# A fused recommendation tower: early casts and a cast-free start of unit 1, moved marks, and 34 idle turns on TensorE before the first lookup

## The reference

```python
e = stack([tbl_f[ids[:, f]] for f in range(26)], axis=1)        # 2048 x 26 x 128
combined = concatenate([dense[:, None, :], e], axis=1)          # 27 vectors of 128
inter = einsum('bfd,bgd->bfg', combined, combined)              # all dot products
z = concatenate([dense, inter[:, iu0, iu1]], axis=1)            # 351 pairs, i < j
h = concatenate([z, dense], axis=1)                             # 128 + 351 + 128 = 607
h = relu(h @ W_top1 + b_top1)                                   # 512
h = relu(h @ W_top2 + b_top2)                                   # 256
y = h @ W_top3                                                  # 1
```

## Time and profile before

| what | value |
|---|---|
| median of 3 runs | 389.83 us (389.62 to 391.64) |
| the profiled execution: time, span | 391.7 us, 390.0 us |
| TensorE busy | 367.0 us, 94% of the span |
| VectorE, ScalarE, GpSimd busy | 268.3, 190.6, 267.1 us |
| mean granted TensorE clock | 0.994 |
| indirect gathers | 278, 953 ns each on GpSimd, median 2.6 us from issue to landing |
| moved | 35.51 MB, mean 91 GB/s |

### The profile page before, as it was taken

The page is one execution under the profiler, slowest core; times in us unless marked ns, Lnnn a source line. Parts: engine busy times, 40 slices in busy tenths (PEclk is TensorE's granted clock), DMA queues, the critical chain, the costliest instruction groups (busy, mean ns, idle before and its releaser), DMA issues.

```text
span 390.0 us, 7774 instructions
## 1 busy us (share of the span) xinstructions
PE 367.0 (94%) x3094; PEld 360.2 (92%) x3094; DVE 268.3 (69%) x275; ACT 190.6 (49%) x424; POOL 267.1 (68%) x287
## 2 busy tenths in 40 slices
PE   1997998799999999999999999999999999999996
PEld 1786987799999999999999999999999999999996
DVE  5698866979686677819686676828687676832451
ACT  1479346356533565346623455436633465426643
POOL 7777767777777777777677777777677777775000
PEclk9999999999999999999999999999999999999999
DMA  6974821444334332433324342343334342321000
GB/s 229 328 213 93 251 84 51 93 90 82 74 82 96 74 95 56 95 81 77 76 76 102 68 103 56 91 87 76 76 70 104 70 96 62 82 56 42 2 2 1
DMA packets 23004, 35.51 MB, mean 91 GB/s; under 512 B 6252, under 2 KB 16748, under 8 KB 22968
## 3 DMA queue, kind: packets, MB, share of 16 engines
q0 software_dynamic: 8896, 18.24, 19.9%
q1 hardware_dynamic: 13976, 16.77, 16.1%
q10 hardware_dynamic: 96, 0.00, 0.0%
HBM read 34.98 MB, written 0.01 MB: 90 GB/s over the span
## 4 chain that ended last, share of the span: by engine, by line
PE 89%; ACT 4%; DVE 4%; issue 2%; DMA 1%; SPq 0%; DVEq 0%
PE l_ps L387 31%; PE g_ps L417 28%; PE t_ps L396 7%; PE h_ps L429 6%; PE h_ps L431 5%; PE h_ps L430 5%; PE l_ps L379 2%; DVE onehot L604 2%; PE h_ps L476 2%; PE t_ps L425 1%; ACT hot_high L731 1%; DMA hot_idx<-in_hot_ids 1%; DVE zf L634 1%; ACT g_ps L738 1%; ACT xT L752 1%
## 5 line engine op out<-in xcount | busy, mean ns | idle before, releaser
L352 POOL DMA_INDIRECT emb<-in_tbl,idx x278 | 264.9, 953 | 89.7 <-issue 74.1
L604 DVE TENSOR_TENSOR onehot<-hot_idx,rows_ps 128x2048 fp32r<-128x2048 int32 x69 | 155.8, 2283 | 7.5 <-PE l_ps L379 3.2
L417 PE MATMUL g_ps<-xT 128*123 128x108 f32 x1024 | 116.6, 271 | 1.6 <-issue 0.8
L417 PEld LDWEIGHTS g_ps<-xT 128*123 128x123 f32 x1024 | 113.7, 188 | 2.0 <-issue 2.0
L387 PE MATMUL l_ps<-onehot,hot_low 128*128 128x256 f32 x528 | 77.7, 290 | 3.6 <-DVE onehot L604 1.7
L387 PE MATMUL l_ps<-onehot,hot_high 128*128 128x256 f32 x528 | 74.8, 285 | 0.0
L772 ACT COPY zg<-g_ps 27x216 f32<-27x216 f32 x160 | 52.6, 329 | 44.9 <-PE g_ps L417 43.8
L387 PEld LDWEIGHTS l_ps<-onehot,hot_low 128*128 128x128 f32 x528 | 68.3, 193 | 5.0 <-ACT xT L752 2.4
L387 PEld LDWEIGHTS l_ps<-onehot,hot_high 128*128 128x128 f32 x528 | 68.9, 194 | 0.0
L752 ACT COPY xT<-l_ps 128x512 f32<-128x512 f32 (+1 forms) x37 | 25.8, 697 | 71.5 <-PE l_ps L387 70.1
L627 DVE COPY zg<-g_ps 27x216 f32<-27x216 f32 x96 | 36.9, 384 | 32.2 <-PE g_ps L417 30.7
(11 more groups left out here) (64 smaller groups left out, 299.1 us busy)
## 6 DMA issues: line engine op xcount, KB each, us to landing
hot_idx<-in_hot_ids SPq DMA_DIRECT2D x69, 128.0 KB, 3.3
stage<-in_hot_tables SPq DMA_DIRECT2D x9, 512.0 KB, 7.0
emb<-in_tbl,idx POOLq DMA_INDIRECT x278, 2.6
dT<-in_dense_t SPq DMA_DIRECT2D x8, 128.0 KB
wz<-in_W_pairs SPq DMA_DIRECT2D x1, 512.0 KB
w2s<-in_W_top SPq DMA_DIRECT2D x1, 512.0 KB
wz<-in_W_dense SPq DMA_DIRECT2D x1, 256.0 KB
wd<-in_W_dense SPq DMA_DIRECT2D x1, 256.0 KB
```

What stands on the lines that cost most here:

```text
L352: pool.indirect_dma_start(emb[:, t % 2, n, :], None, tables[FIELDS[n]][:, :], bass.IndirectOffsetOnAxis(ap=idx[:, t, n:n + 1], axis=0)).th ...
L417: last = pe.matmul(g_ps[c % 2][0:TALL, i, 0:WIDE], four.rearrange("d s f -> d (s f)")[:, 0:TALL], four[:, :, 0:FEATS], start=True, stop=True)
L604: dve.tensor_tensor(onehot[n % ONEHOTS][:], here, rows, ALU.is_equal).then_inc(onehot_ready, 1)
```

## The change

- GpSimd: in unit 1, the gram marks that a gather waits for stop at chunk 4, so gathers that waited for chunks 5 to 8 wait for chunk 4.
- TensorE: once the identity is written, it is turned 34 times into `t_ps`, ahead of `first_unit`; nothing reads the result. In unit 1, lookup 3 comes before the turning of z.
- VectorE: in unit 1, compare 3 comes before the pack; the addition of the dense weights moves from the end of unit 0 to before compare 2 of unit 1.
- ScalarE: tables 0, 1 and 2 are cast first; the dense placement of unit 0 moves ahead of the third hot copy; the casts of the first four weight parts, with their waits, move from unit 1 into unit 0, around the last cold copy.

```diff
--- before.py
+++ after.py
@@ -337,7 +337,8 @@
 
                     k = m // 2 + 1 - (u in LEAN)
                     if k <= 2 * CHUNKS:
-                        pool.wait_ge(gram_done, 2 * CHUNKS * (u - 1) + k)
+
+                        pool.wait_ge(gram_done, 2 * CHUNKS * (u - 1) + (min(k, CHUNKS) if u == 1 else k))
                     else:
                         pool.wait_ge(looked_up, lookups(u) + min(k - 2 * CHUNKS, len(looked(u))))
 
@@ -544,6 +545,9 @@
                 gram(1, CHUNKS - 1)
 
             pe.wait_ge(ident_ready, 1)
+
+            for i in range(34):
+                pe.transpose(t_ps[:, i % 4, :], ident[:], ident[:])
             first_unit()
             for u in range(1, UNITS):
                 even, odd = 2 * u, 2 * u + 1
@@ -556,9 +560,12 @@
                 if u >= 2:
                     layer(u - 2, M1)
                 look_up(u, 2)
-                turn_z(even - 1)
-                look_up(u, 3)
-                if u >= 2:
+                if u == 1:
+                    look_up(u, 3)
+                    turn_z(even - 1)
+                else:
+                    turn_z(even - 1)
+                    look_up(u, 3)
                     layer(u - 2, M1 + 1)
                 turn(even, 2)
                 look_up(u, 4)
@@ -675,8 +682,11 @@
             for u in range(UNITS):
                 even, odd = 2 * u, 2 * u + 1
                 if u:
+                    if u == 1:
+                        one_hot(u, 3)
                     pack(even - 1)
-                    one_hot(u, 3)
+                    if u > 1:
+                        one_hot(u, 3)
                     if u == 1:
                         cut_weights(0)
                         cut_weights(1)
@@ -711,14 +721,13 @@
                 copy_gram(even, 2)
                 copy_gram(even, 3)
                 if u == 0:
+                    dve.wait_ge(w1_landed, 64)
+                    dve.tensor_tensor(wz[:, PQ, :], wz[:, PQ, :], wd2[:], ALU.add).then_inc(wd_summed, 1)
                     one_hot(1, 2)
                 pack(even)
                 copy_gram(odd, 2)
                 cut_z(even)
                 copy_gram(odd, 3)
-                if u == 0:
-                    dve.wait_ge(w1_landed, 64)
-                    dve.tensor_tensor(wz[:, PQ, :], wz[:, PQ, :], wd2[:], ALU.add).then_inc(wd_summed, 1)
             pack(TILES - 1)
             cut_z(TILES - 1)
             for i in range(M1):
@@ -813,7 +822,8 @@
 
             def first_unit():
 
-                table_part(3)
+                for h in range(4):
+                    table_part(h)
                 bank_part(0)
                 table_part(4)
                 copy_hot(0, 0)
@@ -827,13 +837,11 @@
                 copy_cold(0, 1)
                 table_part(7)
                 bank_part(4)
+                place_dense(0)
                 copy_hot(0, 2)
                 copy_cold(0, 2)
                 table_part(8)
                 bank_part(5)
-                for h in range(WHOLE):
-                    table_part(h)
-                place_dense(0)
                 copy_cold(0, 3)
                 bank_part(6)
                 copy_hot(0, 3)
@@ -850,7 +858,14 @@
                 copy_gram(0, 2)
                 copy_gram(0, 3)
                 copy_cold(1, 3)
+                act.wait_ge(w1_landed, 64)
+                weight_part(0)
+                weight_part(1)
                 copy_cold(1, 4)
+                act.wait_ge(wd_summed, 1)
+                weight_part(2)
+                weight_part(3)
+                act.wait_ge(small_landed, 16)
                 for c in range(CHUNKS - 1):
                     copy_gram(1, c)
                 copy_z(0)
@@ -861,20 +876,11 @@
                 even, odd = 2 * u, 2 * u + 1
                 copy_cold(even, 0)
                 copy_hot(u, 0)
-                if u == 1:
-                    act.wait_ge(small_landed, 16)
-                    act.wait_ge(w1_landed, 64)
-                    weight_part(0)
-                    weight_part(1)
                 copy_cold(even, 1)
                 if u >= 2:
                     layer(u - 2, M1)
                 copy_z(even - 1)
                 copy_hot(u, 1)
-                if u == 1:
-                    act.wait_ge(wd_summed, 1)
-                    weight_part(2)
-                    weight_part(3)
                 if u >= 2:
                     layer(u - 2, M1 + 1)
                 copy_cold(even, 2)
```

## The result

The changed kernel takes 388.90 us in the median of 11 runs (386.86 to 390.06), the kernel before 390.01 in as many on the same chip (389.53 to 391.64). The ratio is 0.9954, with a 95% interval of 0.9936 to 0.9972: 1.8 us less, 1.1 to 2.5. The profiled execution took 389.79 with a span of 388.1, 1.9 under the span of before. That is faster, by less than 0.5%; 386.8 had been predicted.

The account below looks back on a forecast made before the run. TensorE's work was taken to bound the kernel from about 78 us, so gains come only by bringing it there sooner. -3.85 - 0.60 + 1.40 = -3.05 off the median 389.83 gave 386.8 us; range 385.0 to 389.6.

Parts of the forecast that it names:

- Unit 0: Up to the first gram: turns and earlier casts start it at 38.1 instead of 41.92, 3.85 us gained.
- rival A: Start of unit 0: the turns don't lift the clock, only the moved casts gain, 2.3; total 388.3 us; chance 0.27.
- TensorE then follows its old order without a new wait, so it keeps the 3.85: After the first gram: TensorE meets no new wait, so the 3.85 us gained in unit 0 lasts.
- Rival C: Unit 0: late list or table 4, or clock lost before first gram, eats 1.5 to 1.8; 388.8 us; chance 0.08.
- The addition's removal: VectorE, unit 1: moving the dense weights' addition out of its chain to the cut of z gains 0.60 us.
- The merged gap: TensorE, unit 1: two gaps become one of 3.1 us, the clock falls, lookups 4 and 5 pay 1.4 us.
- Rival B: Unit 1: the clock does not fall in the merged gap, so -4.45 us, 385.4 us; chance 0.09.
- Rival D: Start: half-clock turns take longer than doubled, delaying the first lookup; slower, at the bound +1.7, 391.5 us; chance 0.06.
- The marks: GpSimd, unit 1: the gathers lose a 2.07 us wait at 57.73, with no gain on the path.
- the spare: Last gather's 3.9 us beyond a median landing before its turn; nearly used up if GpSimd's old marks stayed.
- my -3.05: Whole kernel: the predicted sum, -3.85 in unit 0, -0.60 for the addition, +1.40 for the clock's fall.
- sign of being wrong: Two stated signs: first gram later than 39.6, or TensorE waiting on a gather after 80 us.

## Why the prediction was right in direction, and off in size

**Unit 0: right.** Predicted compare 3 at 14.1, compare 5 at 21.2, last cut ended at 38.0, first gram at 38.1; measured 14.17, 20.95, 37.79, 37.94. The gain there was 3.98 for 3.85. Its parts were less well sized: rival A put the first gram at 39.6 with the casts alone, and without the turns it stood at 38.78, in a trace where the first 32 matmuls began at 8.15 and took 9.08 us, not at 8.48 and 9.68. The turns brought 0.84 there, not 1.5. Rival A, that turns don't lift the clock, is refuted: with nothing but turns before it, the pace doubled at 4.2 us, and 3 us of turns kept the clock at 1.00. The Trainium skill says in "TensorE: Matmul & The Clock Gate", Part 4, that in transpose mode the full clock does not engage. That did not hold for these float32 turns, whose pace went from 0.213 to 0.115 us; the measurement decides. I had taken the rise as 5.3 us after the beginning; it came after 2.8, so the turns ended at 6.87, not 7.9.

**"TensorE then follows its old order without a new wait, so it keeps the 3.85": wrong**, and this is the step that failed. 1.10 us went at 44.99. I had checked the gathers only by their median landing of 2.6 us, at the last turn, where 3.9 were spare. Under the weights' transfers the gather of 37.16 needed 7.3 us in the kernel before: landed at 44.5, it was some 3.3 us ahead of its turn at 47.87, less than the gain of 3.98. In the changed kernel it needed 7.7, another 0.4, and 3.98 - 3.3 + 0.4 = 1.1. Rival C named the right fate (eaten in front) at the wrong place: unit 0's clock did not fall. That its 388.8 is within 0.1 of the median is luck, and its own terms (1.5 to 1.8 off the 3.05) give 388.3 to 388.6.

**Unit 1: right.** The addition's removal gave 0.50 for 0.60 (from 2.83 ahead at 52.69 to 3.33 at 69.69). The merged gap lasted 3.16 us (3.1 predicted), the clock fell, and the fall cost 1.41 for 1.40. That this agrees so closely is partly luck, since the price was picked between 0 and 2.6. The fall is in all four traces with the merged gap empty (2.95 to 3.16 us), and from the third turn to lookup 5's second half it cost 1.4 to 1.5 in each against those where the clock held; without the turns and with the old marks it reaches into lookup 5, which the table's last column doesn't show. Rival B is refuted for these executions; for the three of the changed kernel with a mean clock of 0.998 or 0.999 it may hold. Rival D is refuted by the first lookup at 8.29.

**The marks: nothing**, as predicted, but for another reason than the spare: the fifth chunk is now done before the gather's own queue reaches it. That the spare would nearly be used without this edit was wrong.

**The sum.** -3.98 at the first gram, +1.10 at the gather, +0.05 up to the grams at 52.69, -0.50 in VectorE's chain, +1.41 by the clock: -1.92; the span says -1.9. Missing from my -3.05 is the gather's wait. Neither sign of being wrong came: the first gram was not later than 39.6, and TensorE waited on no gather after 80 us.

**The base of the forecast.** This sum compares two profiled executions in both of which the clock fell (mean 0.994 each). The prediction took its 3.05 off the median of before, 389.83, but in the profiled execution lookup 8 lost 1.77 us to the clock just before the first gram, and the median execution may not have had that loss to give back. Of the 55 executions of before on the other chips, 29 have a mean clock of 0.998 or 0.999 and take 389.24 to 390.80, the other 26 have 0.994 to 0.996 and take 390.66 to 391.87, some 1.2 us more. No trace of one of the first kind was kept, so what the change brings there is not shown. The range reached to 389.6 for rivals A and C, and 388.90 lies in it for a reason that neither of them names.

What the parts are worth thus depends on one another: the turns 0.3 us, which is within the noise, in the changed kernel and 1.8 where the gather is in time and the gap filled; the casts 2.3 there.

## What to carry to other kernels

When an edit moves an engine forward by some microseconds, check every wait behind it with the latency that its transfer had in that stretch, not with the median over the run: a burst of weights nearly tripled it here. When two idle stretches of TensorE are merged, the sum may drop the clock where neither did; fill the gap with turns, or leave work between. A gain measured as small may be a larger one with losses behind it: taking away both turned 1.8 us into 3.9, while either alone stayed within the noise. And when executions of one kernel fall into groups, look which group the profiled one belongs to before its trace is set against a median.

## What the runs showed of the hardware

TensorE's turns of a 128 x 128 identity raise its clock from 1.2 to 2.4 GHz and hold it there, read from their pace: 0.213 us a turn before the rise (2.77 us for 13), 0.115 at full clock (3.00 us for 26 in the filled gap). The rise came 2.8 us after the first turn in the profiled execution of the changed kernel; with the turns alone, 34 took 6.77 us instead of 5.44, so it came later there.

Gathers issued while 1.75 MB of weights were in transfer landed after 7.0 to 7.7 us in the changed kernel; with the weights issued early, the two issued between 36.5 and 37.6 us landed after 2.8.

Executions of one program differ in their mean granted clock, and the time goes with it: of the changed kernel, three at 0.998 or 0.999 took 386.86 to 388.37 us, the eight at 0.991 to 0.996 took 388.39 to 390.06. Filled, or with its two gaps kept apart, and the gather in time, the kernel took 386.41 to 387.38 at 0.997 or more.
